# Four experts per product and the gate weights applied by VectorE, in a kernel of a Mamba layer, dense experts, attention and routed experts

## The reference, cut to what matters

```python
K = 2
logits = x @ Wg.T + bg
w = softmax(logits)                 # over the 8 experts
top, idx = top_k(w, K)              # two experts per token
y = sum over e of gate[token, e] * (x[token] @ W[e].T + b[e])
x = layernorm(x + y)
```

## Time and profile before

| | |
|---|---|
| median of 3 runs | 1549.94 us (1544.75 to 1559.22) |
| the profiled execution's own time | 1547.93 us |
| its span in the profile | 1546.2 us |
| TensorE busy | 1418.8 us (92%), mean granted clock 0.952 |
| VectorE busy | 1075.2 us (70%) |
| ScalarE busy | 863.1 us (56%) |
| GpSimd busy | 275.4 us (18%) |

### The profile page before, as it was taken

How to read it: one execution, slowest core, us unless ns; L and a number is a source line. 1 busy time by engine, 2 the same in 40 slices (tenths; PEclk the granted TensorE clock), 3 DMA queues, 4 the chain that set the end, 5 groups by cost and what they waited for, 6 DMA issues and landing times.

```text
span 1546.2 us, 21289 instructions
## 1 busy us (share of the span) xinstructions
PE 1418.8 (92%) x7543; PEld 635.6 (41%) x7543; DVE 1075.2 (70%) x2056; ACT 863.1 (56%) x1751; POOL 275.4 (18%) x409
## 2 busy tenths in 40 slices
PE   6998998899788988999999999999999999985786
PEld 3655665575556553222223232233322333322353
DVE  7766568738755577888887879888888888843023
ACT  6554235415531322677777777777777767773142
POOL 2211121102111203000000110501104111043452
PEclk9989899889979988999999999999999999998898
DMA  4080000200010922111101111011101100000135
GB/s 122 9 197 14 1 1 14 100 1 1 29 72 1 165 100 100 36 22 21 22 2 22 39 22 22 26 25 40 22 14 26 26 1 2 1 5 26 42 99 172
DMA packets 47343, 64.45 MB, mean 42 GB/s; under 512 B 9730, under 2 KB 34893, under 8 KB 45398
## 3 DMA queue, kind: packets, MB, share of 16 engines
q1 hardware_dynamic: 44166, 58.84, 14.9%
q0 software_dynamic: 3072, 4.25, 0.8%
HBM read 33.08 MB, written 32.03 MB: 42 GB/s over the span
## 4 chain that ended last, share of the span: by engine, by line
PE 59%; DVE 6%; ACT 2%; issue 2%; POOL 1%; DMA 1%; DVEq 0%; ACTq 0%; POOLq 0%
PE ps L591 57%; DVE smax L2046 2%; PE ps L584 1%; ACT space L1417 1%; POOL expert_in L1609 1%; DVE st L1759 1%; ACT space L1438 0%; PE ps L940 0%; DVE x_all L1777 0%; ACT space L1459 0%; PE ps L1072 0%; DMA shift_rows<-shiftT 0%; DMA space<-expert_in 0%; DVE x L1995 0%; DVE mv L1764 0%
## 5 line engine op out<-in xcount | busy, mean ns | idle before, releaser
L591 PE MATMUL ps<-space 128*32 128x512 f32 (+5 forms) x4608 | 846.7, 476 | 33.5 <-DVE space L1901 14.2
L2046 DVE TENSOR_REDUCE smax<-ps 128x1 f32<-128x1024 f32 x512 | 605.1, 1219 | 119.1 <-PE ps L591 113.0
L1417 ACT ACTIVATE space<-ps 128x512 f32<-128x512 f32 x1024 | 555.2, 595 | 211.1 <-PE ps L591 210.5
L591 PEld LDWEIGHTS ps<-space 128*32 128x32 f32 (+5 forms) x4608 | 248.6, 109 | 604.7 <-ACT space L1417 328.9
L1510 POOL TENSOR_SCALAR eps_sum<-mv 128x4 f32<-128x4 f32 x32 | 7.3, 229 | 615.1 <-DVEq L1766 614.6
L1272 ACT ACTIVATE btok<-ps 128x128 f32<-128x128 f32 x32 | 8.9, 277 | 148.4 <-PE ps L591 68.1
L591 PE MATMUL ps<-ones,ident 128*128 128x512 bf16 x271 | 73.1, 423 | 15.9 <-POOLq L1613 12.3
L591 PE MATMUL ps<-w_exp,space 128*128 128x128 f32 x512 | 81.5, 311 | 0.0
L591 PEld LDWEIGHTS ps<-w_exp,space 128*128 128x128 f32 x512 | 69.8, 213 | 16.1 <-issue 15.9
L1860 DVE SCALAR_TENSOR_TENSOR space<-space,conv_w 128x512 f32<-128x512 f32 x96 | 71.1, 750 | 2.3
L1609 POOL DMA_INDIRECT expert_in<-space,slot x64 | 62.9, 982 | 36.3 <-issue 19.3
(11 more groups left out here) (252 smaller groups left out, 1487.7 us busy)
## 6 DMA issues: line engine op xcount, KB each, us to landing
q_rows<-space SPq DMA_DIRECT2D x24, 256.0 KB, 2.4
k_rows<-space SPq DMA_DIRECT2D x24, 256.0 KB, 2.9
space<-k_rows SPq DMA_DIRECT2D x16, 384.0 KB, 5.3
space<-q_rows SPq DMA_DIRECT2D x16, 384.0 KB, 7.0
expert_out<-x_all SPq DMA_DIRECT2D x2, 2048.0 KB, 21.3
space<-expert_out SPq DMA_DIRECT2D x4, 1024.0 KB, 8.6
v_rows<-space SPq DMA_DIRECT2D x4, 668.0 KB, 3.6
space<-v_rows SPq DMA_DIRECT2D x4, 668.0 KB, 6.6
```

Of the source, the lines that this page charges most:

```text
L591: return nc.tensor.matmul(out, lhsT, rhs, start=first, stop=last)
L1417: nc.scalar.activation(prob[:, QUAD * (step % PROB_SETS) + unit % QUAD, :], bank(STB + unit % 2), ACT.Exp)\
L2046: v.tensor_reduce(smax[:, N % 2, i:i + 1], ps[:, b0:b0 + 2, :].rearrange("p k n -> p (k n)"), AX.X, ALU.max).then_inc(S.s_max, 1)
```

## The change

The gates are no longer applied to the inputs on their way into TensorE. TensorE multiplies one tile of 128 tokens by four experts at once: the tokens (`xnT`, 128x128) are the weights, and `w_exp` of four experts, 512 columns, streams through. So a product holds in one bank, for 128 tokens, the outputs of four experts, not gated. VectorE adds them to `x2` out of PSUM, one expert of one tile at a time, with the gate as the scalar of each token: 64 instructions of 128x128 per batch. The products come in eight pairs k: two tiles of tokens, and experts 0 to 3 for even k, 4 to 7 for odd k. The biases are one product per half with the gates turned in a single transpose, against a table `b_exp` of 64 x 1024 that holds the biases of each tile on its own columns. `g3`, `pick_rows`, `xs` and their steps go, and with them the copy of `pick_rows` by ScalarE in slot 0.

In TensorE's order a pair stands ahead of `chunk_out` (`PRODUCTS_AHEAD`) or behind it (`PRODUCTS_BEHIND`), the last one after `mix_out(m, 1)`. The `keep_clock` calls among the sums in slots 1 to 3 go; slot 4 has one of 10 at c = 2 and one of 8 at c = 3. The pairs of scores 0 and 1 are issued at c = 2 there. At the end of a slot VectorE does `mix_norm(m, 0)` and `mix_variance(m, 1)` ahead of the last pair.

```diff
-SUMS_AT = {4: (0, 1, 2), 5: (3, 4, 5, 6), 6: (7, 8, 9, 10), 7: (11, 12)}
-SUMS_LAST = (13, 14, 15)
+EXPERT_BANKS = (6, 7), (4, 5), (6, 7), (6, 7), (6, 7), (4, 5), (6, 7), (5, 6)
+PRODUCTS_AHEAD = {3: 1, 4: 2, 5: 3, 6: 4, 7: 6}
+PRODUCTS_BEHIND = {2: 0, 6: 5}
+SCALED_AT = {3: (0,), 4: (1, 2), 5: (3,), 6: (4, 5), 7: (6,)}
+BIAS_AT, LAST_PAIR = 5, 7
-PAIRS_IN_SUMS = {1: 2, 3: 3, 5: 4, 8: 5, 11: 6, 13: 7}
-MAXIMA_IN_SUMS = {0: 0, 1: 1, 3: 2, 5: 3, 7: 4, 11: 5, 13: 6, 15: 7}
+PAIRS_IN_SUMS = {1: 2, 2: 3, 3: 4, 4: 5, 5: 6, 6: 7}
+MAXIMA_IN_SUMS = {0: (0, 1), 2: (2,), 3: (3,), 4: (4,), 5: (5,), 6: (6,), 7: (7,)}
...
             def mix_out(b, H):
...
+                    if b >= 1:
+                        pe.wait_ge(S.experts_used, 2 * E * (b - 1) + 12)
...
             def gates_turned(b):
                 pe.wait_ge(S.gsel_ready, b + 1)
+                pe.wait_ge(S.experts_used, 2 * E * b + 4)
+                nc.tensor.transpose(bank(5)[0:NT * E, 0:P], gsel[:].rearrange("p t e -> p (t e)"), ident[:]).then_inc(S.gT_psum, 1)
+            def expert_biases(b):
+                pe.wait_ge(S.gT_sb, b + 1)
+                for H in range(2):
+                    mm(bank(4 + H), gT, b_exp[:, half(H)]).then_inc(S.bias_psum, 1)
+            def expert_pair(b, k):
+                if k == 0:
+                    pe.wait_ge(S.xnT_ready, turned("moe", b) + 2)
+                    pe.wait_ge(S.route_shift, 2 * b + 1)
+                elif k == 5:
+                    pe.wait_ge(S.moe_added, 2 * b + 2)
+                elif k >= 2:
+                    used = {2: 2, 3: 6, 4: 8, 6: 10, 7: 14}[k]
+                    pe.wait_ge(S.experts_used, 2 * E * b + used)
+                for w in range(2):
+                    mm(bank(EXPERT_BANKS[k][w]), tile(xnT, 2 * (k // 2) + w),
+                       w_exp[:, HT * (k % 2):HT * (k % 2) + HT, :].rearrange("p e d -> p (e d)")).then_inc(S.experts_psum, 1)
...
# TensorE, the loop over c
+                    if p is not None and c == BIAS_AT:
                         gates_turned(p)
-                        if m is not None:
-                            keep_clock(OUTB, 5)
+                    if p is not None and c in PRODUCTS_AHEAD:
+                        if m is None and c == 3:
+                            keep_clock(5, 8)
+                        expert_pair(p, PRODUCTS_AHEAD[c])
+                        if m is None and PRODUCTS_AHEAD[c] in PAIRS_IN_SUMS:
+                            score_pair(PAIRS_IN_SUMS[PRODUCTS_AHEAD[c]])
                     if m is not None:
                         chunk_out(m, c)
...
-                        if m is not None and HT <= c < NT - 1:
-                            keep_clock(OUTB, 2)
-                        for k in SUMS_AT.get(c, ()):
-                            expert_sum(p, k)
...
+                        if c == 2 and m is None:
+                            keep_clock(YB, 10)
+                            score_pair(0)
+                            score_pair(1)
+                        if c == BIAS_AT:
+                            expert_biases(p)
+                        if c in PRODUCTS_BEHIND:
+                            expert_pair(p, PRODUCTS_BEHIND[c])
...
                 if m is not None:
                     mix_out(m, 1)
                 if p is not None:
+                    expert_pair(p, LAST_PAIR)
...
# VectorE
+            def bias_added(b):
+                dve.wait_ge(S.experts_used, 2 * E * b + 8)
+                for H in range(2):
+                    dve.wait_ge(S.bias_psum, 2 * b + H + 1)
+                    v.tensor_tensor(x2[:, own(H), :], x2[:, own(H), :], tiles4(4 + H), ALU.add).then_inc(S.moe_added, 1)
+            def experts_scaled(b, k):
...
+                elif k == 4:
+                    dve.wait_ge(S.moe_added, 2 * b + 2)
+                else:
+                    dve.wait_ge(S.experts_used, 2 * E * b + 2 * k)
+                dve.wait_ge(S.experts_psum, 2 * E * b + 2 * k + 2)
+                earlier = {}
+                for e in range(HT):
+                    for w in range(2):
+                        i = 2 * (k // 2) + w
+                        if e:
+                            mine.wait(earlier[w])
+                        ins = v.scalar_tensor_tensor(x2[:, i, :], tiles4(EXPERT_BANKS[k][w])[:, e, :],
+                                                     gsel[:, i, HT * (k % 2) + e:HT * (k % 2) + e + 1], x2[:, i, :],
+                                                     ALU.mult, ALU.add)
+                        if e < HT - 1:
+                            earlier[w] = mine.mark(ins)
+                        else:
+                            ins.then_inc(S.experts_used, 1)
...
                     if p is not None:
-                        for k in SUMS_AT.get(c, ()):
-                            expert_step(p, k)
+                        for k in SCALED_AT.get(c, ()):
+                            experts_scaled(p, k)
+                            if c == BIAS_AT:
+                                bias_added(p)
+                                expert_statistics(p, 0)
                             if m is None and k in MAXIMA_IN_SUMS:
-                                pair_max(MAXIMA_IN_SUMS[k])
+                                for pair in MAXIMA_IN_SUMS[k]:
+                                    pair_max(pair)
...
                 if m is not None:
                     mix_norm(m, 0)
                     mix_variance(m, 1)
                 if p is not None:
-                    expert_added(p, 1)
+                    experts_scaled(p, LAST_PAIR)
+                    if m is None:
+                        for pair in MAXIMA_IN_SUMS[LAST_PAIR]:
+                            pair_max(pair)
+                if p is not None:
+                    expert_statistics(p, 1)
                 if m is not None:
                     mix_norm(m, 1)
```

More of the change, by code:

```diff
@@ L156, in build @@
         w_exp = sb("w_exp", [P, E, D])
[L157 to L158 removed]
+        b_exp = sb("b_exp", [NT * E, NT * D])
         w_route0 = sb("w_route0", [P, E])
@@ L785, in gates_turned @@
                 pe.wait_ge(S.gsel_ready, b + 1)
-                for n in range(NT):
-                    last = nc.tensor.transpose(bank((7, 5)[n // HT])[0:E, (n % HT) * P:(n % HT + 1) * P], gsel[:, n, :], ident[:])
-                last.then_inc(S.gT_psum, 1)
-                pe.wait_ge(S.g3_ready, 3 * b + 3)
-                for n in range(NT):
-                    last = nc.tensor.transpose(bank(6)[0:3 * E, :].bitcast(BF16)[:, n * P:(n + 1) * P],
-                                               g3[:, n].rearrange("p s e -> p (s e)"), ident16[:])
@@ L793, in gates_turned @@
-                last.then_inc(S.g3T_psum, 1)
-            def gate_rows(b, k):
-                H, e = k // E, k % E
-                if k == 0:
-                    pe.wait_ge(S.late_ready, N_LATE)
-                    pe.wait_ge(S.g3T_sb, b + 1)
-                elif k == 1:
-                    pe.wait_ge(S.gT_sb, b + 1)
-                else:
-                    pe.wait_ge(S.xs_ready, 2 * E * b + k - 1)
-                mm(bank(6 + k % 2), pick_rows[:, e, :], g3T[:, half(H)]).then_inc(S.gate_rows, 1)
@@ L1260, in evac_gates @@
                 act.wait_ge(S.gT_psum, b + 1)
-                for H in range(2):
-                    last = nc.scalar.activation(gT[:, half(H)], bank((7, 5)[H])[0:E], ACT.Copy)
-                last.then_inc(S.gT_sb, 1)
+                nc.scalar.activation(gT, bank(5)[0:NT * E, 0:P], ACT.Copy).then_inc(S.gT_sb, 1)
             def chunk_copy(b, c):
@@ L1352, in _ @@
                         decays_so_far(m, c + 2)
-                    if p is not None and c == HT:
+                    if p is not None and c == BIAS_AT:
                         evac_gates(p)
@@ L2133, in _ @@
                         gate(m, c // 2)
-                if p is not None:
-                    for k in SUMS_LAST:
-                        expert_step(p, k)
-                        if m is None and k in MAXIMA_IN_SUMS:
-                            pair_max(MAXIMA_IN_SUMS[k])
                 if m is not None:
@@ L2350 @@
     qkv_order = np.concatenate([by_dim, D + by_dim, 2 * D + np.arange(D)])
+    biases = np.zeros((NT, E, NT, D), np.float32)
+    for i in range(NT):
+        biases[i, :, i, :] = x["L0_ffn_b"]
     arrays = {
```

94 lines of the change are left out of this document (15 added, 79 removed).

## The result

The changed kernel takes 1538.74 us (median of 20 runs, 1530.70 to 1550.72), the kernel before 1549.97 (20 runs, 1540.72 to 1559.22). The ratio is 0.9934, 95% interval 0.9914 to 0.9955: a gain of 11.2 us where 22 were forecast. On two further chips the ratio was 0.9936 (0.9907 to 0.9965) and 0.9948 (0.9926 to 0.9971). The 20 runs fall into two groups, twelve from 1530.7 to 1539.4 us with a mean granted clock of 0.946 to 0.955, and eight from 1545.0 to 1550.7 us with 0.937 to 0.943; the profiled run, 1545.66 us, is of the upper one, so I read stages from it and the total from the medians.

What follows compares the result with a forecast made beforehand. TensorE's in-order work was taken to bound chunks 4 to 6 while VectorE waits. Gains of 35.2 us, less 10.5 for clock, plus 1.0, less 3.5 for handoffs, made 22: 1549.9 to 1528 us, range 1511 to 1545.

Steps and rivals of the forecast that it cites:

- three stretches at full clock, before less new: Slots 1 to 3, carry of chunk 4 to last mix norm: 57.6, 58.7, 56.7 us before, 43.9 new.
- A: From VectorE's carry of chunk 4 to `mix_out(m, 0)`: 23.8 us forecast, 38.5 before.
- B: From `mix_out(m, 0)` to `mix_out(m, 1)`: 9.9 us forecast, 8.6 before.
- C: From `mix_out(m, 1)` to the end of the last mix norm: 10.2 us forecast, 10.4 before.
- entry to the stretch, three slots: Ahead of the stretch, pair 0 costs 1.2 us in slots 1 and 3, 3.7 in slot 2.
- further handoffs: Some ten more handoffs per slot at about 0.1 us that the parts leave out: 3.5 us.
- the clock: Idle times of about 3 us before each `mix_out` cost 3.5 us per slot, 10.5 in all; bounds nothing to 8.6 per slot.
- slot 4 and what follows, to attention: Slot 4 from gates to last statistics: 30.3 us against 32.1, a gain of 1.8, taken as 1.
- Pitch and place of the scaling: VectorE's 64 new instructions per batch start 0.262 us apart, a pair in 2.10; bounds 0.23 and 0.38.
- serial rival: Waits in VectorE's 64 new instructions cost like ones on the direct predecessor: pitch 0.38, 1559 us, slower; chance 0.08.
- clock rival: Both gaps drop the clock in each slot, 8.6 us instead of 3.5: 1545 us; chance 0.18 with partial forms.
- The norms ahead of the last pair: First mix norm runs under `mix_out(m, 1)`; GpSimd gets its variances earlier, and nobody waits for that longer than now.

Runs made afterwards that it cites:

- half_scaling: Changed kernel with four of each pair's eight VectorE scaling instructions left out in slots 1 to 3: 1512.91 us, ratio 0.9769 to the kernel before.
- clock_both_gaps: Changed kernel with twelve idle products in each of TensorE's two waits before the mix_outs, slots 1 to 3: 1557.02 us, ratio 0.9811 to the kernel before.
- before_no_fill: Kernel before without its 14 idle products per slot between the expert sums of chunks 4 to 7, slots 1 to 3: 1557.18 us, ratio 1.0065.

## Why the prediction was off

By its own steps, up to the start of attention, where the profile has a gain of 622.53 - 615.06 = 7.5 us:

| step | taken | measured |
|---|---|---|
| three stretches at full clock, before less new | 41.3 | A, B, C at full clock 24.1 + 10.2 + 10.5 per slot |
| entry to the stretch, three slots | -6.1 | -4.9 |
| further handoffs | -3.5 | -4.2 |
| the clock | -10.5 | -26.8 |
| slot 4 and what follows, to attention | +1.0 | +2.0 |
| sum | 22.2 | 7.4 |

- **Pitch and place of the scaling: right.** Taken 0.262, measured 0.267, a pair in 2.16 us. The serial rival (0.35 or more) is refuted. The prediction set a rule of the Trainium skill against the row ("VectorE: DVE Perf Modes", section on the DRAIN), that the next instruction waits until the pipe is empty. It left out that the same paragraph goes on to say that a next instruction that is not held starts earlier, and the trace agrees with that: instructions of 341 ns start 267 ns apart. The sign of VectorE's busy share was set at over 90% in chunks 4 to 6; it was 82 and 86%, with 0.88 us of waiting for ScalarE per chunk. That VectorE's scaling sets the pace there is shown by half_scaling.
- **Lengths at full clock: right.** 23.8, 9.9 and 10.2 were worked out; clock_both_gaps has 24.1, 10.1 to 10.4, and 10.5. What they miss, 24.1 + 10.2 + 10.5 - 43.9 = 0.9 per slot, is 2.7 of the handoff term; 1.5 more came once, in slot 1's part A, where the clock stood at 0.92 (pair 3 took 2.97 us there behind a wait of 1.83, and 1.98 behind the same wait in slots 2 and 3): 4.2 against 3.5.
- **The clock: wrong, and this is the step that failed.** The prediction saw both waits, took the price of one fall as 4.3 us and of two as 8.6, and then chose 3.5 per slot, "nearer to one fall than two". All three slots show both falls: B and C take 88.9 us in the first profile and 62.0 with the waits filled, 26.8 in all or 8.9 per slot. The profile of clock_both_gaps is from another chip; against the control beside it, 84.9 us, it is 22.9 or 7.6 per slot. So the value lay at the upper bound, at 7.6 to 8.9, and the term of 10.5 was 12 to 16 us too small. At half clock the output product became 1.9 times as long (6.82 against 3.64) and the pair up to 2.1 times, where 1.8 was taken for both. One reason given for less was small products around the fall in slots of the old kernel. It was no evidence for the new slots: before_no_fill shows that fourteen idle products per slot were holding part of that clock up. In the first profile the difference is 16.3 us. It, less 1.2 and 1.0 that the entry and slot 4 did better and plus 0.7 of handoffs, is 14.8, the 22.2 less the 7.4.
- **A fall behind one such wait stood in the trace of before.** The prediction sets a price of 8.6 because it finds no pair of such gaps in a slot, and says that the rows at 0.50 agree with what it cites on utilization. But the earlier trace rows shows TensorE busy throughout at 0.50 and not what stood ahead. In slot 2 that is a single wait of 2.99 us; the group behind it takes 0.69 us, where it takes 0.44 at the high clock (204.21 in the earlier trace rows):

```profile
290.83 0.69 PE L591 MATMUL ps<-space 128*64 128x128 f32 x4 [2.99 <-DVE space L1901]
```

- **The clock rival: right in mechanism.** It said 1545; the median is 1538.7, between it and the forecast. The median lies inside the stated range because the range reached to this rival, not because the forecast's sum was right. Its sign (a start of attention less than 10 us earlier) came true. It got 0.18 because two waits of 3 us in each slot were known and their effect was treated as open. Of the 7.5 us at the start of attention 2.3 are left at the end of that profile. Most of the loss is in the routed experts: at a wait of 12.3 us that both kernels have (ending at 1429.0 and 1435.3) the gain is still 6.2, and the granted clock of a stretch of 30 us behind it (from 1432.5 and from 1440) is 0.86 against 0.98. No run took it apart. The median gain is 11.2, and no step explains what lies between.
- **The norms ahead of the last pair: right as written, but not weighed.** "Nobody waits for that longer than now" holds: in the kernel before the first norm ended at 214.9 us and the last at 219.6, and ScalarE's squares stood behind it as well. What the prediction did not see is ScalarE's queue, and so what this order is worth: undone, it costs 15.6 us, more than the whole gain, and the dense experts would have bought nothing that can be measured (1.0022). The order avoids a loss that the new pair would have brought.
- **Slot 4.** From the gates to the last statistics 31.7 us against 32.1: 0.4 of the calculated 1.8. The rest of the 2.0 lies around it, and no run took it apart.

## What to carry to other kernels

When a change turns TensorE's steady small work into dense products, list the waits that it leaves and price each at full effect, for everything that TensorE does until the clock is back; here a fall cost 3.1 to 5.1 us over the three profiles of the changed kernel, on top of a wait of about 3. Look in the old trace for a wait of the same length, and read what the clock did behind it. Fill such a wait with products that are due anyway before filling it with idle ones: the second buys back the clock, the first the clock and the work. And when an instruction is moved, follow its result into the queues of the engines that read it: what stands behind the reader in that queue pays as well.

## What the runs showed of the hardware

- A TensorE wait of 2.96 to 3.32 us was followed by half clock, at once or some 2 us after work resumed, in every B and C of the changed kernel's first profile; B and C were 13.2 us or longer behind all 18 such waits (2.81 to 3.32 us) of its three profiles. Behind 0.70 to 0.76 us the kernels with pairs in the waits kept the high clock in B and C of all slots. Behind 1.38 to 1.39 us half_scaling had B at 9.6 us twice and at 12.9 once; behind its waits of 2.47 us C took 12.6 to 14.3. Before pair 3 each slot of the changed kernel has a wait of 1.83 us: behind it the pair took 1.98 or 1.99 us seven times in the three profiles, and 2.97 and 3.55 in slot 1 of two of them. At half clock an output product of 3.57 to 3.64 us took up to 6.82, a pair of 1.72 up to 3.55.
- Raising the clock need not gain: in a stretch of chunk 1 it went from 0.52 to 1.00 with ten idle products, and TensorE's next wait grew from 0.69 to 2.99 us.
- The time of a kernel differs by 2.4 to 2.7% between chips (before: 1549.97, 1547.23, 1587.03 and 1588.94 us). Most of it lies behind the start of attention: on the two slower chips TensorE stands still in the attention loops four to six times, for 1.5 to 8.2 us each, in every kernel, in about half of them with nothing named that it waited for, and with ScalarE named in the others. The timeline of the changed kernel on the third chip:

```profile
985.82 2.01 PE L587 MATMUL ps<-space 128*32 128x512 f32 x9
996.04 3.87 PE L587 MATMUL ps<-space 98*128 98x512 bf16 x12 [8.22 <-issue]
```

On the two faster chips the attention loops have no stop of 1.5 us or more. What causes these stops stays open. A ratio is taken within one chip, so both of its kernels have them.
